# Moving the first hidden unit of the next expert ahead of the last output tile in a mixture-of-experts loop

## The reference, cut to what matters

```python
def _moe(t, ...):                       # t: (2048, 1024), E = 8 experts, I = 2048
    w = gate weights of the top 2 experts of each token, else 0      # (2048, 8)
    def body(acc, ew):
        w1, b1, w2, b2, we = ew
        h = _swiglu(t @ w1 + b1)        # w1: (1024, 4096), even columns glu, odd columns lin
        y = h @ w2 + b2                 # w2: (2048, 1024)
        return (acc + we[:, None] * y, None)
    acc, _ = jax.lax.scan(body, acc0, (mlp1_w, mlp1_b, mlp2_w, mlp2_b, w.T))

def _swiglu(h):
    x_glu = jnp.minimum(h[..., ::2], 7.0)
    x_lin = jnp.clip(h[..., 1::2], -7.0, 7.0)
    return x_glu * jax.nn.sigmoid(1.702 * x_glu) * (x_lin + 1.0)
```

## Time and profile before

| what | us |
|---|---|
| median of the runs | 4880.86 (two runs: 4728.74 and 5032.98) |
| the profiled execution | 4679.42, of which the span of the slowest core is 4677.9 |
| spans of the 8 cores in it | 4608.8 to 4677.9, granted TensorE clock 0.841 to 0.849 |
| TensorE busy with matmuls, slowest core | 3733.3 (80% of the span) |

### The profile page before, as it was taken

How to read it: one execution, slowest core, us unless ns; L and a number is a source line. 1 busy time by engine, 2 the same in 40 slices (tenths; PEclk the granted TensorE clock), 3 DMA queues, 4 the chain that set the end, 5 groups by cost and what they waited for, 6 DMA issues and landing times.

```text
span 4677.9 us, 43587 instructions; the slowest of 8 cores (4608.8 to 4677.9 us)
## 1 busy us (share of the span) xinstructions
PE 3733.3 (80%) x15475; PEld 1571.6 (34%) x15475; DVE 2361.0 (50%) x3093; ACT 737.1 (16%) x1342; POOL 229.8 (5%) x375
## 2 busy tenths in 40 slices
PE   0565775775774799899899989837999999999996
PEld 0222112112112344344344434323444444444442
DVE  3455445544546646355355454466463463554554
ACT  0140540540550001001011010000010010010010
POOL 1101001000000000000000000000000000000000
PEclk9858558558555799999999999957999999999998
DMA  5404004002003235325434344131253253244240
GB/s 118 37 1 36 1 1 36 1 1 27 1 1 54 32 45 95 63 55 90 68 58 81 54 82 72 29 80 29 45 99 72 46 99 63 54 90 72 54 90 36
DMA packets 146178, 242.07 MB, mean 52 GB/s; under 512 B 74280, under 2 KB 74280, under 8 KB 145968
## 3 DMA queue, kind: packets, MB, share of 16 engines
q0 software_dynamic: 139040, 222.34, 29.6%
q1 hardware_dynamic: 4624, 8.56, 0.7%
q10 hardware_dynamic: 2304, 8.39, 0.5%
HBM read 453.19 MB, written 8.39 MB: 99 GB/s over the span
## 4 chain that ended last, share of the span: by engine, by line
PE 56%; DMA 6%; DVE 5%; issue 1%; DVEq 1%; ACT 0%; POOL 0%; ACTq 0%; POOLq 0%
PE psY L897 20%; PE psY L855 17%; PE psA L855 9%; PE psB L855 8%; DMA w1l<-wlin 6%; PE psY L730 1%; DVEq L87 1%; PE psY L713 1%; DVE t2fm L717 1%; DVE psY L871 0%; DVE gfm L720 0%; DVE he L876 0%; DVE psY L874 0%; DVE u2b L686 0%; DVE u2b L917 0%
## 5 line engine op out<-in xcount | busy, mean ns | idle before, releaser
L897 PE MATMUL psY<-w2b,he 128*128 128x512 bf16 x4096 | 912.8, 387 | 66.6 <-DVE he L876 66.6
L897 PEld LDWEIGHTS psY<-w2b,he 128*128 128x128 bf16 x4096 | 406.0, 99 | 573.4 <-issue 108.7
L855 PE MATMUL psA<-t2fm,w1g 128*128 128x512 bf16 x2048 | 495.0, 398 | 99.2 <-DMA w1l<-wlin 96.0
L905 DVE SCALAR_TENSOR_TENSOR acc<-psY,wgate,acc 128x1024 f32<-128x1024 f32 x128 | 164.4, 1284 | 773.9 <-PE psY L897 773.9
L855 PE MATMUL psY<-t2fm,w1g 128*128 128x512 bf16 x2048 | 462.9, 379 | 0.0
L855 PE MATMUL psY<-t2fm,w1l 128*128 128x512 bf16 x2048 | 462.9, 379 | 0.0
L855 PE MATMUL psB<-t2fm,w1l 128*128 128x512 bf16 x2048 | 462.9, 379 | 0.0
L863 ACT ACTIVATE psA<-psA,b1gt 128x1024 f32<-128x1024 f32 x128 | 139.5, 1090 | 1720.3 <-PE psA L855 1720.2
L855 PEld LDWEIGHTS psA<-t2fm,w1g 128*128 128x128 bf16 x2048 | 206.8, 102 | 370.0 <-issue 150.7
L548 PE MATMUL psO<-attnT,vbuf 128*64 128x512 bf16 x448 | 231.9, 528 | 100.4 <-ACT attnT L537 99.9
L868 DVE TENSOR_SCALAR u2b<-psA 128x1024 f32<-128x1024 f32 x128 | 156.8, 1225 | 284.0 <-ACT psA L863 284.0
(11 more groups left out here) (161 smaller groups left out, 3201.9 us busy)
## 6 DMA issues: line engine op xcount, KB each, us to landing
w2b<-w POOLq DMA_DIRECT2D x32, 2048.0 KB, 22.8
w1g<-wglu POOLq DMA_DIRECT2D x128, 512.0 KB, 6.1
w1l<-wlin POOLq DMA_DIRECT2D x128, 512.0 KB, 8.4
wqk<-wqkv POOLq DMA_DIRECT2D x64, 256.0 KB, 5.4
xres<-x SPq DMA_DIRECT2D x4, 2048.0 KB, 30.7
y<-xres ACTq DMA_DIRECT2D x16, 512.0 KB, 5.3
wvb<-wqkv POOLq DMA_DIRECT2D x8, 256.0 KB, 19.4
woutb<-wout POOLq DMA_DIRECT2D x8, 256.0 KB, 42.2
```

The lines of the kernel that those rows point to most:

```text
L855: c.op("tensor", lambda e, wsrc=wsrc, pdst=pdst, kc=kc, t=t, hc=hc, buf=buf: e.matmul(pdst[:, t * 512:(t + 1) * 512], wsrc[buf][:, kc * 25 ...
L897: c.op("tensor", lambda e, py=py, hc=hc, t=t, i=i: e.matmul(py[:, t * 512:(t + 1) * 512], he[:, hc * 1024 + i * 128:hc * 1024 + (i + 1) * ...
L905: c.op("vector", lambda e, py=py, i=i, e_=e_: e.scalar_tensor_tensor(acc[:, i * D:(i + 1) * D], py[:, :], wgate[:, i * E + e_:i * E + e_ + 1],
```

## The change

The body of the unit loop becomes a function `m1_unit(e_, u, mm_only, sw_only)`. For experts 1 to 7, unit 0 is no longer part of the unit loop. Its matmuls (with their waits) are put on TensorE's queue between output tiles 6 and 7 of the expert before; its Silu and its four VectorE operations follow the eviction of output tile 7, with one more wait on VectorE, for the matmuls of output tile 7, ahead of the write into `he`. This happens 7 times in each half, 14 times in all. The number of matmuls, of operations and of transfers stays the same, and the text of `load_piece` and of the `w2b` load is not changed.

```diff
-                for u in range(HC):
+                def m1_unit(e_, u, mm_only=False, sw_only=False):
                     p, hc = u // 2, u % 2
                     hg = u
                     buf = (e_ * NP + p) % 2
                     pr = pairs[u % 2]
                     wsem1, wval1 = R[("w1ld", h, e_, p)]
-                    c.wait("tensor", wsem1, wval1)
+                    if not sw_only:
+                        c.wait("tensor", wsem1, wval1)
...
-                    for (wsrc, pdst) in ((w1g, pr[0]), (w1l, pr[1])):
-                        for kc in range(KC):
-                            for t in range(2):
...
-                    R[("m1mm", h, e_, u)] = c.n("s_pe")
+                    if not sw_only:
+                        for (wsrc, pdst) in ((w1g, pr[0]), (w1l, pr[1])):
+                            for kc in range(KC):
+                                for t in range(2):
...
+                        R[("m1mm", h, e_, u)] = c.n("s_pe")
+                    if mm_only:
+                        return
                     c.wait("scalar", "s_pe", R[("m1mm", h, e_, u)] - 1)
...
                     c.op("vector", lambda e, pr=pr: e.tensor_scalar(
                         pr[1][:, :], pr[1][:, :], -LIMIT, 1.0, OP.max, OP.add))
+                    if sw_only:
+                        c.wait("vector", "s_pe", R[("m2mm", h, e_ - 1, 7)])
                     c.op("vector", lambda e, pr=pr, hg=hg: e.tensor_tensor(
                         he[:, hg * 1024:(hg + 1) * 1024], u2b[:, :], pr[1][:, :], OP.mult),
                         inc=("s_ve", 1))
...
+                for u in range(1 if e_ > 0 else 0, HC):
+                    m1_unit(e_, u, sw_only=(u == 0 and False))
...
                     R[("m2ev", h, e_, i)] = c.n("s_ve")
+                    if i == 6 and e_ + 1 < E:
+                        m1_unit(e_ + 1, 0, mm_only=True)
+                    if i == 7 and e_ + 1 < E:
+                        m1_unit(e_ + 1, 0, sw_only=True)
```

More of the change, by code:

```diff
@@ L851, in walkB @@
                         c.wait("tensor", "s_ve", R[("accb", h, 7)])
-                    for (wsrc, pdst) in ((w1g, pr[0]), (w1l, pr[1])):
-                        for kc in range(KC):
-                            for t in range(2):
[L855 to L860, removed]
-                    R[("m1mm", h, e_, u)] = c.n("s_pe")
+                    if not sw_only:
+                        for (wsrc, pdst) in ((w1g, pr[0]), (w1l, pr[1])):
+                            for kc in range(KC):
+                                for t in range(2):
+                                    c.op("tensor", lambda e, wsrc=wsrc, pdst=pdst, kc=kc, t=t, hc=hc, buf=buf: e.matmul(
+                                        pdst[:, t * 512:(t + 1) * 512],
+                                        wsrc[buf][:, kc * 256 + hc * 128:kc * 256 + (hc + 1) * 128],
+                                        t2fm[:, kc * 1024 + t * 512:kc * 1024 + (t + 1) * 512],
+                                        start=(kc == 0), stop=(kc == KC - 1)),
+                                        inc=("s_pe", 1) if (kc == KC - 1 and t == 1) else None)
+                        R[("m1mm", h, e_, u)] = c.n("s_pe")
+                    if mm_only:
+                        return
                     c.wait("scalar", "s_pe", R[("m1mm", h, e_, u)] - 1)
```

## The result

The changed kernel takes 4795.2 us (median of 11 runs), the kernel before 4704.9 (median of 10, five of them 4668 to 4681). Both medians contain runs in which one die or both held a lower TensorE clock; the ratio, and the times of runs further down, leave those out. The ratio is 1.022, with a 95% interval of 1.018 to 1.027. So the change makes the kernel slower by 2.2%, some 105 us: by all likelihood more than 2%, but the interval reaches just under that bound. The profiled execution of the changed kernel took 4784.7 us, its span is 4783.2 us on core 4, against 4679.4 and 4677.9.

What follows compares the result with a forecast made beforehand. TensorE, busy for 80% of the span, was taken to bound the kernel. The late w2b's 96.6 us, other terms at nothing, gave 4776 from 4679.4 and 4825 from 4728.7; point about 4801 us, range 4735 to 4985.

Steps and rivals of the forecast that it cites:

- Where the bubble is, and what it hangs on: No bubble at the expert seam; unit 4 waits for piece 2, behind w2b, on average 6.86 us.
- rival 1: Piece 2 lands as much earlier as it is issued: 1.7 us per boundary, 24 us in all; 4%.
- rival 4: Unit 1's new wait for the eviction is not hidden: 24 us on top, effect 121 us; 2%.
- rival 3: Transfers run faster with TensorE idle: 0.5 us per boundary, 7 us in all, no change; 3%.
- rival 2: Time from tile 7's end to unit 4 shifts: effect 44 to 80 us 15%, over 120 us 11%.
- (b): Tile 7's end (T') comes 6.90 us later, and w2b and unit 4 with it: 14 x 6.90 = 96.6 us.
- (a): Unit 0's 32 matmuls ahead of tile 7: 6.90 us each way, no work saved; their waits can't stop tile 7.
- (c): Unit 1 waits for tile 7's eviction: 1.7 us per boundary, 24 us, in front of the DMA bubble, cost nothing.
- (d): Unit 0's swiglu behind tile 7's eviction on VectorE: hidden, with 1.6 us in hand before unit 2.
- (e): Unit 4's slow first matmuls after the bubble: 1.7 to 2.4 us already paid, not growing; nothing taken for it.
- The rate of the queue: Loads at 436 GB/s would mean 26 us, no bubble before and an 85 us change; trace disagrees, not used.
- against which time: Sum gives 4776 from the profiled 4679.4, 4825 from the run at 4728.7; point at their middle, about 4801.

Runs made afterwards that it cites:

- late piece 2: Kernel before, with piece 2 of experts 1 to 7 issued after unit 2 and not after unit 1: ratio 0.999 (0.994 to 1.003).
- cut `w2b`: Kernel before, w2b of experts 1 to 7 in four 1 MB transfers, one behind each of pieces 2 to 5: ratio 0.978, again 0.976.
- half unit: Changed kernel, only unit 0's 16 glu matmuls ahead of tile 7, the 16 lin matmuls behind it: ratio 1.0114 to the kernel before.
- covered version: Changed kernel, unit 1 waiting for tile 7's eviction only ahead of its lin half: 4784.7 to 4794.5 us, again 4770.1 and 4773.7.

## Why the prediction was right, and where not

**Where the bubble is, and what it hangs on.** Right. The seam had no bubble, and unit 4 waits for piece 2 behind `w2b`. The late piece 2 and the cut `w2b` show it from both sides. Rivals 1 and 4 fall by the runs above, and so does rival 3 (L would have been 6.4 us shorter; it wasn't). Of rival 2 no more came than 0.45 us of L, see (b).

**(a) The moved matmuls.** Right: tile 7 follows unit 0 without a wait at 3440.23.

**(b) 14 x 6.90 = 96.6 us for the late `w2b`.** Right in kind and nearly in size. The prediction has piece 2 go out at T' + 9.3 in this step and at T' + 9.9 in rival 1; 9.9 is what the trace shows, since the eviction wait delays unit 1, and nothing hangs on it. The half unit gave 53 us, and putting `w2b` behind the pieces took some 80 of the 105 us away. Read off all 14 boundaries of the slowest core, from the end of tile 7 to the start of unit 4, L averages 34.9 us (30.9 to 38.3), where it averaged 34.5 in the kernel before (30.4 to 38.5). That is 14 x 0.45 = 6.3 us, and with the 2.0 us ahead of the loop it accounts for 8.3 of the 8.7 us by which the span grew beyond the sum. L falls in the course of the kernel mostly because the load of `w2b` gets shorter: in the kernel before, from the issue of its first transfer to the landing of its second, it takes 31.5 us at the first boundary and 24.7 at the last. Why it does is open.

**(c) The eviction wait, 14 x 1.7 us at no cost.** Its size was right (22.3 us). That it is hidden is shown by the 14 DMA waits behind it, the shortest 8.5 us, while the covered version alone leaves it open; it has its full price, about 22 us, once the DMA wait is gone. The DMA wait should have been 170 us by the prediction and was 174.9.

**(d) The swiglu behind the eviction.** Right: no wait for it, and with the matmuls left in place the rest of the change was without a visible effect.

**(e) The surcharge after the bubble.** It did not grow with the wait. After 14.39 us of idle time at the first boundary unit 4's 16 glu matmuls take from 1794.01 to 1800.05, 6.0 us; by the same count they take 5.9 after the 6.12 us of the earlier trace rows, and 3.45 at full pace. Over the 14 boundaries the surcharge averages 2.1 us, and 1.9 in the kernel before. The groups behind the new wait of 1.5 to 2.1 us keep their full pace.

**The rate of the queue.** The 436 GB/s of the Trainium skill (DMA: Bandwidth & Descriptors, Anatomy of one DMA) gave L = 26.8 and no bubble before; the trace had the bubble. The distance is mostly in `w2b`: in the changed kernel its transfers land 17.0 us and, counted from an issue 0.9 us later, 27.1 us after their issues, so 11.0 us apart for 4.2 MB read, some 380 GB/s; over the 14 boundaries it is 9.9 to 13.4 us, 420 to 310 GB/s. The transfers of piece 2 come near the rate of the Trainium skill, with 2 x 1.05 MB in 5.0 us, 420 GB/s. The 168 to 216 GB/s of the earlier trace rows don't contradict this: over the 30 us they make some 5.6 MB, near the 5.24 MB of bf16 that are written and not the 10.5 MB that are read.

**The step that failed: against which time.** The sum stood against the profiled execution and gave 4776 us, an effect of 2.1%. That was right: the measured ratio is 1.022, some 105 us. I then set the point at the middle of 4776 and 4825, 4801, because of a run at 4728.7, and left it beside a shown median of 4880.9. Read against that median, 4801 is a gain of 1.6%, while the argument said a loss of 2%, and the measurement shows a loss of 2.2%. The further runs of the kernel before show that the profiled execution was the level to build on: five of ten lie at 4668 to 4681, and the 4728.7 was the odd one, though such runs come back: two of 11 in the later measurements lie at 4708 and 4725. The comparable runs of the change lie at 4774 to 4807, with 4785 in their middle. The sum of 4776 was at their foot, and the absolute point with its range should have come with the level of before that it supposes. That the stated 4801 came within 6 us of the measured median of 4795.2 is luck: the 25 us by which it stands above the sum come from the one odd run, and the median from the mix of runs. The chances, 54% for over 2% and 44% for within, were as near the edge as the measurement turned out to be.

## What to carry to other kernels

Before moving work, ask what waits for the end of what it is moved ahead of, the DMA issues too, and follow that wait to where TensorE really stands still; here it was four units later. A move is worth something only in front of a wait. And in one queue of transfers, put the small load that is wanted soon ahead of the large one that is wanted late: this, with the large load cut in four, gave 2.2 to 2.4%, about as much as the change lost.

## What was not expected of the hardware

The eight cores of the kernel before end 69 us apart. With `w2b` cut, and not a matmul changed, they end within 7 us of each other:

```profile
core 5: 4555.2 us, clock 0.848
core 6: 4561.5 us, clock 0.846
```

These are the fastest and the slowest. The cores' programs are the same, so the spread came through the DMA wait: between cores of one execution it varied from 43.8 to 96.0 us. It goes with `w2b` itself: its second transfer takes 23.7 us from issue to landing on core 1, the mean of the 14 boundaries, and 27.2 on core 7, and 14 x 3.55 is 50 of the 52 us. The rest of the 69 us is mostly the surcharge behind the wait, 0.8 us on average on core 1 and 1.9 on core 7. Why one core's load takes longer than another's was not tried.
